# The exponential of an attention unit in two pieces of 1024 and 512 columns, the partial sums added by GpSimd

## The reference

```python
# block 0: one head of 64
attention = jax.nn.softmax(jnp.einsum('bik,bjk->bij', q, k), axis=-1)
attended = jnp.einsum('bij,bjk->bik', attention, v)
# block 1: two heads of 32
attn = jax.nn.softmax(jnp.einsum('bhld,bhmd->bhlm', q, k) * SCALE, axis=-1)
out = jnp.einsum('bhlm,bhmd->bhld', attn, v)
# block 3: four heads of 16, with relative positions
score = (content_score + rel_shift(pos_score)) / np.sqrt(D)
ctx = jnp.einsum('bhst,bthd->bshd', jax.nn.softmax(score, axis=-1), v)
```

## Time and profile before

| What | Value |
|---|---|
| Median of 3 runs | 5632.31 us (5630.87 to 5649.04) |
| Profiled execution, its own time | 5644.55 us |
| Span of the profiled execution | 5642.7 us |
| TensorE busy | 4372.6 us, 77% |
| VectorE busy | 3331.4 us, 59% |
| ScalarE busy | 1815.6 us, 32% |
| GpSimd busy | 425.7 us, 8% |
| Mean granted TensorE clock | 0.822 of full speed |

### The profile page before, as it was taken

How to read it: one execution, slowest core, us unless ns; L and a number is a source line. 1 busy time by engine, 2 the same in 40 slices (tenths; PEclk the granted TensorE clock), 3 DMA queues, 4 the chain that set the end, 5 groups by cost and what they waited for, 6 DMA issues and landing times.

```text
span 5642.7 us, 71238 instructions
## 1 busy us (share of the span) xinstructions
PE 4372.6 (77%) x26536; PEld 2924.2 (52%) x26536; DVE 3331.4 (59%) x9075; ACT 1815.6 (32%) x2723; POOL 425.7 (8%) x484
## 2 busy tenths in 40 slices
PE   6886755799888755699888755699887765699987
PEld 4554544555646534555546534555546544555646
DVE  4444769555545669555555669555555659655554
ACT  2232521144332522134332422134332421234432
POOL 0100000011100000011100000021100000011100
PEclk9898865699988975599988975699988975689988
DMA  2000000000000000000000000000000000000000
GB/s 80 3 3 15 1 16 1 1 1 1 1 1 4 1 16 1 1 1 1 1 1 4 1 16 1 1 1 1 1 1 4 1 1 1 1 1 1 1 1 4
DMA packets 28309, 26.48 MB, mean 5 GB/s; under 512 B 10550, under 2 KB 26934, under 8 KB 27450
## 3 DMA queue, kind: packets, MB, share of 16 engines
q1 hardware_dynamic: 27962, 21.98, 1.4%
HBM read 20.40 MB, written 1.57 MB: 4 GB/s over the span
## 4 chain that ended last, share of the span: by engine, by line
PE 49%; DVE 29%; issue 5%; POOL 4%; ACT 3%; DVEq 1%; SPq 0%; POOLq 0%; ACTq 0%
PE ps L581 10%; PE ps L615 7%; DVE qup L759 4%; PE ps L1584 3%; DVE x L757 3%; PE ps L1600 3%; DVE x L761 3%; DVE ctxt L802 3%; PE ps L642 3%; DVE ctxt L798 2%; POOL st L394 2%; PE ps L915 2%; PE ps L414 2%; PE ps L427 2%; DVE row_max L1047 2%
## 5 line engine op out<-in xcount | busy, mean ns | idle before, releaser
L615 PE MATMUL ps<-cst,big 128*128 128x128 f32 x4608 | 674.9, 298 | 345.0 <-ACT big L717 312.5
L615 PEld LDWEIGHTS ps<-cst,big 128*128 128x128 f32 x4608 | 570.1, 154 | 426.3 <-ACT big L717 354.9
L698 ACT COPY big<-ps 128x512 f32<-128x512 f32 x816 | 478.6, 586 | 877.1 <-PE ps L615 877.1
L832 DVE TENSOR_REDUCE negmax<-ps 128x1 f32<-128x1536 f32 x336 | 590.1, 1757 | 64.0 <-PE ps L588 44.8
L717 ACT ACTIVATE big<-ps,negmax 128x1536 f32<-128x1536 f32 x336 | 518.7, 1544 | 269.0 <-DVE negmax L832 269.0
L409 PE MATMUL ps<-cst 128*128 128x512 f32 x608 | 332.5, 707 | 127.4 <-DVEq L187 58.2
L394 POOL TENSOR_TENSOR st<-st,cst 128x6 f32<-128x6 f32 x104 | 156.8, 1508 | 3449.3 <-DVE st L382 3445.2
L581 PE MATMUL ps<-kup,qup 128*128 128x512 f32 (+3 forms) x768 | 358.1, 563 | 41.8 <-POOLq L187 41.0
L588 PE MATMUL ps<-qlo 128*128 128x512 f32 x576 | 343.9, 736 | 7.4 <-DVEq L187 7.4
L422 ACT COPY xt<-ps 64x512 f32<-64x512 f32 x144 | 80.7, 579 | 828.0 <-PE ps L414 828.0
L642 PE MATMUL ps<-big,v 128*32 128x128 f32 (+1 forms) x8064 | 324.7, 278 | 8.1 <-DVE ctxt L1071 6.0
(11 more groups left out here) (317 smaller groups left out, 7131.4 us busy)
## 6 DMA issues: line engine op xcount, KB each, us to landing
rw<-in_w_route SPq DMA_DIRECT2D x128, 64.5 KB, 1.8
cst<-in_consts SPq DMA_DIRECT2D x1, 2671.0 KB, 14.7
cst<-in_consts SPq DMA_DIRECT2D x1, 2670.5 KB, 8.8
big<-in_consts SPq DMA_DIRECT2D x1, 1872.5 KB, 22.0
out_dram<-res SPq DMA_DIRECT2D x4, 384.0 KB, 2.8
experts_in<-in_consts SPq DMA_DIRECT2D x1, 1360.0 KB, 17.5
qup<-in_patches SPq DMA_DIRECT2D x4, 260.0 KB
klo<-in_pe_low SPq DMA_DIRECT2D x2, 384.0 KB, 23.3
```

The lines of the kernel that those rows point to most:

```text
L615: ins = nc.tensor.transpose(turned_bank(kind, u, g)[:, i * P:(i + 1) * P], prob[:, slot_of(kind, u), (4 * g + i) * P:(4 * g + i + 1) * P], ...
L698: copy(pt[:, slot_of(kind, u), g, 0:n], turned_bank(kind, u, g)[:, 0:n]).then_inc(*ph.mark(copier(kind, g)))
L832: nc.vector.tensor_reduce(negmax[:, u:u + 1], flat[:, 0:n], AX.X, ALU.max, negate=True)\
```

## The change

In attn0, attn1, attn3a and attn3b the exponential is two instructions, for columns 0 to 1023 and 1024 to 1535, each with its own accumulated sum in `part_sum` and its own signal. The transposes of groups 0 and 1 wait for the first, those of group 2 for the second. GpSimd adds the two sums into `rowsum`, one unit behind its copy into `qz`, and now does so in attn0 and attn1 as well; VectorE's reciprocal waits for that. attn2 stays as it was.

```diff
@@ SIGNALS, in attn0 (attn1, attn3a and attn3b alike, with 48 and 24)
-    "probs_ready": 12,
+    "probs_ready": 24, "rows_summed": 12,
@@
         rowsum = sb("rowsum", [P, 48])
+        part_sum = sb("part_sum", [P, 48, 2])
@@
         def attn_pool(ph, pool, kind):
-            link = pool_chain(ph, pool)
+
             for u, (hd, q) in enumerate(units_of(kind)):
-                if u >= 2:
-                    pool.wait_ge(*ph.after("side_ready", u - 1))
-                nc.gpsimd.tensor_copy(qz[64:80, u % 2, :], qlo[64:80, hd % 2, q * P:(q + 1) * P]).then_inc(*ph.mark("queries_alone"))
-                pool.wait_ge(*ph.own("queries_alone"))
+                if kind.startswith("attn3"):
+                    if u >= 2:
+                        pool.wait_ge(*ph.after("side_ready", u - 1))
+                    nc.gpsimd.tensor_copy(qz[64:80, u % 2, :], qlo[64:80, hd % 2, q * P:(q + 1) * P])\
+                        .then_inc(*ph.mark("queries_alone"))
+                    pool.wait_ge(*ph.own("queries_alone"))
+                if u >= 1:
+                    sum_rows(ph, pool, u - 1)
+            sum_rows(ph, pool, len(units_of(kind)) - 1)
+
+        def sum_rows(ph, pool, u):
+
+            pool.wait_ge(*ph.after("probs_ready", 2 * (u + 1)))
+            nc.gpsimd.tensor_tensor(rowsum[:, u:u + 1], part_sum[:, u, 0:1], part_sum[:, u, 1:2], ALU.add)\
+                .then_inc(*ph.mark("rows_summed"))
+            pool.wait_ge(*ph.own("rows_summed"))
@@ turn(u, g)
-                if g == 0:
+                if kind == "attn2" and g == 0:
                     pe.wait_ge(*ph.after("probs_ready", u + 1))
+                elif kind != "attn2" and g != 1:
+                    pe.wait_ge(*ph.after("probs_ready", 2 * u + 1 + g // 2))
@@ exps(u)
-                nc.scalar.activation(prob[:, slot_of(kind, u), 0:n], src, ACT.Exp, bias=bias,
-                                     accum_out=rowsum[:, u:u + 1]).then_inc(*ph.mark("probs_ready"))
+                if kind == "attn2":
+                    nc.scalar.activation(prob[:, slot_of(kind, u), 0:n], src, ACT.Exp, bias=bias,
+                                         accum_out=rowsum[:, u:u + 1]).then_inc(*ph.mark("probs_ready"))
+                    return
+                for k, cols in enumerate((slice(0, 1024), slice(1024, S))):
+                    nc.scalar.activation(prob[:, slot_of(kind, u), cols], src[:, cols], ACT.Exp, bias=bias,
+                                         accum_out=part_sum[:, u, k:k + 1]).then_inc(*ph.mark("probs_ready"))
@@ give(u)
-                dve.wait_ge(*ph.after("probs_ready", u + 1))
+                dve.wait_ge(*(ph.after("probs_ready", u + 1) if kind == "attn2" else ph.after("rows_summed", u + 1)))
@@ GpSimd's stream, attn0 (attn1 alike)
-                Phase(led, "attn0").leave(pool)
+                ph = Phase(led, "attn0")
+                attn_pool(ph, pool, "attn0")
+                ph.leave(pool)
```

More of the change, by code:

```diff
@@ L53 @@
         "v_psum": 2, "vec_step": 13, "var_ready": 2, "normed": 1},
-    "attn0": {"strips_ready": 12, "strips_copied": 12, "probs_ready": 12, "pt_by_act": 24, "scores_ready": 12, "pt_psum": 36, "ctx_ready": 12,
+    "attn0": {"strips_ready": 12, "strips_copied": 12, "probs_ready": 24, "rows_summed": 12, "pt_by_act": 24, "scores_ready": 12, "pt_psum": 36, "ctx_ready": 12,
         "max_ready": 12, "pt_by_vec": 12, "vec_step": 12, "ctx_copied": 12},
@@ L62 @@
         "v_psum": 2, "vec_step": 12, "var_ready": 2, "normed": 1, "low_ready": 12},
-    "attn1": {"strips_ready": 24, "strips_copied": 24, "probs_ready": 24, "pt_by_act": 48, "scores_ready": 24, "pt_psum": 72, "ctx_ready": 24,
+    "attn1": {"strips_ready": 24, "strips_copied": 24, "probs_ready": 48, "rows_summed": 24, "pt_by_act": 48, "scores_ready": 24, "pt_psum": 72, "ctx_ready": 24,
         "max_ready": 24, "pt_by_vec": 24, "vec_step": 24, "ctx_copied": 24},
@@ L76 @@
         "bias_ready": 1, "var_ready": 4, "normed": 1, "v_copied": 1, "k_copied": 6, "rot_ready": 6},
-    "attn3a": {"strips_ready": 24, "strips_copied": 24, "queries_alone": 24, "probs_ready": 24, "pt_by_act": 48, "scores_ready": 24, "side_ready": 24,
+    "attn3a": {"strips_ready": 24, "strips_copied": 24, "queries_alone": 24, "probs_ready": 48, "rows_summed": 24, "pt_by_act": 48, "scores_ready": 24, "side_ready": 24,
         "pt_psum": 72, "ctx_ready": 24, "vec_step": 48, "side_read": 24, "max_ready": 24, "pt_by_vec": 24,
@@ L81 @@
         "rot_psum": 6, "k_copied": 6, "rot_ready": 6},
-    "attn3b": {"strips_ready": 24, "strips_copied": 24, "queries_alone": 24, "probs_ready": 24, "pt_by_act": 48, "scores_ready": 24, "side_ready": 24,
+    "attn3b": {"strips_ready": 24, "strips_copied": 24, "queries_alone": 24, "probs_ready": 48, "rows_summed": 24, "pt_by_act": 48, "scores_ready": 24, "side_ready": 24,
         "pt_psum": 72, "ctx_ready": 24, "vec_step": 48, "side_read": 24, "max_ready": 24, "pt_by_vec": 24,
@@ L1170, in _ @@
                 ph.leave(pool)
-                Phase(led, "attn1").leave(pool)
+                ph = Phase(led, "attn1")
+                attn_pool(ph, pool, "attn1")
+                ph.leave(pool)
                 ph = Phase(led, "moe1")
```

## The result

The changed kernel takes 5560.87 us (median of 5 runs, 5535.23 to 5566.83) against 5632.31 us (median of 5 runs, 5630.04 to 5654.71); the ratio is 0.9854, 95% interval 0.9823 to 0.9885. By the ratio, which is taken of means, that is 1.5% or 82 us faster (65 to 100 by the interval); the two medians lie 71 us apart. The forecast was 0.8% or 44 us, and the median is outside the range of 5571 to 5610. A second set of runs of the same kernel gave the same ratio, with medians 85 us apart. In what follows a gain in us is the ratio's, where nothing else is said.

The account below looks back on a forecast made before the run. TensorE's wait for the exponential was taken as reachable in attn1, bound by a loop through ScalarE and TensorE; 35.4 us there plus 8.6 at entries and ends made 44.0, from 5632.31 to 5588.3 us, range 5571 to 5610.

Parts of the forecast that it names:

- attn2's share: TensorE's waits for the exponential in the sparse attention: 63.6 us per pass, 254 us over four passes, untouched by the change.
- The unit of attn1: attn1 in steady state: 3.74 us falls to 3.38, set by VectorE's loop, 0.36 us less per unit; not under 3.30.
- 35.4: Gain forecast in attn1, in us: 8.9 per pass over four passes, from steady state, entry and end.
- The 16 entries and ends of the relative attentions: attn3a and attn3b: eight entries and eight ends, where TensorE's idle time is cut by 0.43 us each.
- the rival in which GpSimd stops VectorE: attn1: addition stops VectorE 0.29 us, bound 3.67, time 5613; twice that, 5639. No measurable gain, shared with late piece: 0.06.
- The second piece: Rival in attn1: a gap before the second piece makes it late; at 0.4 us, unit 3.60, time 5607 us; chance 0.11.
- The pieces: ScalarE's two exponentials per unit: 1024 and 512 columns, recorded at about 1.12 and 0.69 us in the new profile.
- The estimate by the Trainium skill: ScalarE: about 0.3 us per ACTIVATE plus 0.83 ns per element, 1.15 us for the first piece; the forecast kept to the rows.
- the loop of 3.45 us: attn1's ScalarE and TensorE loop by the skill's estimate, 3.31 by the rows; it would pass VectorE's and lose some 6 us.
- the clock stays up: Rival at relative attention ends: full clock kept, 10 us more gained, 13 with the context behind, time 5575; chance 0.07.
- the sum that left it out: Whole-kernel gain: 35.4 us in attn1 plus 8.6 at entries and ends elsewhere, 44.0 us.

Follow-up runs that it names:

- the short maximum: Changed kernel with attn1's row maximum over the first 1024 columns only: 5599.33 us, executed once, attn1's unit from 3.41 to 3.31 us; in the kernel before, it stays 3.74.
- all_but_rel_last: The change, but with the whole exponential in the last unit of each relative attention: ratio 0.9912 (0.9887 to 0.9938) against the kernel before.
- rel_last_only: Kernel before, with the exponential in two pieces only in the last unit of each relative attention, 8 of 336 units: ratio 0.9965, median 5611.89 us against 5629.77.

## Why the prediction was wrong

**What held.** The waits were placed rightly: attn2's share out of reach, attn1's in reach. The unit of attn1 was forecast at 3.38 us and measured at 3.41, with VectorE on the loop that sets it, as the short maximum shows; attn1 gave 33.4 to 33.8 us of 35.4. attn0 gave 2.3 us for 1.7. In steady state attn0 (5.77 us) and the relative attentions (5.84 us) are unchanged: TensorE's transposes there still start without idle time. The 16 entries and ends of the relative attentions gave their 0.43 us each. GpSimd costs nothing in the units, also at four times the work, so the rival in which GpSimd stops VectorE fell. Of the contention that the GPSIMD Engine Reference of the Trainium skill (Specifications) describes, no run here shows any; VectorE reads PSUM at that time. The second piece came early, not late: it starts 0.09 us after the read of the first accumulator begins (623.68 and 623.77), where the forecast had 0.20. The pieces take 1.117 and 0.681 us, forecast at 1.12 and 0.69. The estimate by the Trainium skill (ScalarE: Activation LUTs, Rules for kernel authors) had 1.15 us for the first, near its recorded length; but the next instruction starts 0.10 us before that length is over, and the loop of 3.45 us that I worked out from it did not come.

**The step that failed** is the rival "the clock stays up", and with it the sum that left it out. It had 0.07 and it is what happened. The argument against it, that the first idle stretch of 1.27 us stays, was wrong: that stretch alone does not bring the clock down. In the 13 profiles in which the second stretch is gone (in one of them the first as well), 104 of 104 last transposes ran in 1.53 us; in the 5 with both stretches, 4 of 40 did. The sum put this term at nothing, and it measured 13 us at the ends alone. Its price was short as well. At each end 1.60 us are gained from the last transposes to the next stage (7.33 to 5.73), 12.8 us in eight, as priced at 13; but rel3b behind attn3a gets 5.9 us, and the stages behind attn3b some 7.5 us (1463.0 us in the mean of the five profiles with slow ends, 1455.5 in the 13 others). The last figure holds on average only: all_but_rel_last, with slow ends, has 1458.6 us there, and rel_last_only, with fast ones, 1460.0. The prediction stopped the effect at the end of the stage.

**The second omission** is moe1 and sim2: 62.9 us per pass in the five profiles with a whole exponential in attn1, 60.5 in the seven of the change and its near relatives with a unit of 3.41 us, some 10 us in all. They are untouched, and so I never asked about them.

The sum as measured: 34 in attn1, 2 in attn0, 7 from the waits of the relative attentions, 13 from the clock at their ends, 6 in rel3b, 7 behind attn3b, 10 in moe1 and sim2: 79 of 82 us. The first three make 43, where 44 was forecast. Of the 26 that follow, the 19 at the ends and in rel3b are TensorE's clock, shown by the runs, and the 7 behind attn3b go with it on average; the last 10 show in the clock too, with their cause open. None of these 36 was in the forecast.

**Open:** why the rest of the stages differ from execution to execution (moe2 and rel3a took 462 us in one profile of the change and 480 in the other), and what decides the clock at the entry of moe1 beside TensorE's idle time in attn1.

## What to carry to other kernels

When a change removes a wait on TensorE, look at the granted clock on both sides of it and in the next stage: eight waits of 0.43 us were worth 20 us here (11 to 28), because the clock no longer fell behind them. Where a profile shows a half-clock stretch at the end of a stage, price the whole stretch, into the stages behind, as a case of its own with a real chance, and don't argue it away by one idle time that remains. And split an operation on the path for its first consumer only where the engine behind it is truly waiting: of 336 units only the 96 of attn1 gained from it in steady state, and the gain ended at the next engine, 0.03 us from where the rows had put it.

## What was not expected of the hardware

- At the end of a relative attention, idle stretches of 1.27 and 0.47 us with 0.4 us of work between them brought the granted clock to 0.50, with slow transposes in 36 cases of 40 (5 profiles); 1.27 us alone did not, in 96 cases of 96 (12 profiles). Two idle matmuls in the longer stretch, which took the place of both, kept it up in 8 of 8.
- Two accumulating activations in a row overlap: the second starts 0.09 us after the first one's accumulator read begins, although the read is 0.20 us long. By the page ScalarE's busy time rose from 1815.6 to 1894.7 us, 0.24 us for each of 336 units, not 0.36.
- A float32 matmul of 128x512 costs 0.86 us at full clock, in two records of 0.43; counting one record halves its price. The scores of attn1, which the code casts to F32R, have the same shape in the rows and are one record each (651.22, 0.48 us).
- A reciprocal of 0.16 us on the engine that sets the unit cost nothing, since that engine's loop ran through TensorE at this point.
